# A local-attention transformer on eight cores: wqkv loaded in one piece per row block, and the W1 loop interleaved with its LayerNorm

## The reference, cut

```
x = layernorm(x + attention(x, Wq, Wkv, Wo))          # causal, 16 heads, 2048 tokens, width 1024
y = x
for l in range(2):
    h = shift_token(y)                                # columns 512..1023 shifted by one token
    q, k, v = split(h @ wqkv[l], 3)                   # 3 x 512
    q, k = rotary(l2norm(q) * qs, l2norm(k) * ks)
    y = y + local_attention(q, k, v, window 512) @ wo[l]
    h = layernorm(shift_token(y)) * g + b
    a, g = split(h @ w1[l] + b1, 2)                   # 2 x 2730
    y = y + (a * gelu(g)) @ w2[l] + b2
out = layernorm(x + y)
```

## Time and profile before

| what | us |
|---|---|
| runs | 4656.06 and 4775.8, median 4715.93 |
| the profiled execution | 4707.03 |
| its span, slowest core (7) | 4705.1 |
| TensorE matmuls busy | 3161.8 (67%) |
| VectorE, ScalarE, POOL busy | 1513.8 (32%), 1018.1 (22%), 408.8 (9%) |
| DMA queues | 118.13 MB moved, mean 25 GB/s |
| first QKV matmul, layers 0 and 1 | at 1350.9 and 2958.4 |
| W1 loop, half 0 and half 1 of layer 0, start | at 2293.95 and 2656.63 |
| W1 loop, half 0 and half 1 of layer 1, start | at 3905.7 and 4361.3 |

### The profile page before, as it was taken

One profiled execution on the slowest core, in us unless ns is written; L12 is line 12 of the kernel. 1 busy time (PEld: TensorE's weight loads), 2 busy tenths in 40 slices (PEclk: granted clock), 3 DMA queues, 4 the chain that ended last, 5 costly groups with the idle time before them and its releaser, 6 DMA issues.

```text
span 4705.1 us, 43223 instructions; the slowest of 8 cores (4644.6 to 4705.1 us)
## 1 busy us (share of the span) xinstructions
PE 3161.8 (67%) x11488; PEld 1080.7 (23%) x11488; DVE 1513.8 (32%) x3019; ACT 1018.1 (22%) x1209; POOL 408.8 (9%) x449
## 2 busy tenths in 40 slices
PE   3656566666436667777579696566777765884996
PEld 1212121121112222222134242122222212331341
DVE  1322322212224444444311421344444452124213
ACT  0022435355111222222110110212222211101111
POOL 0000000000022200000020020222000001100110
PEclk9866677788667755556689698676555567875786
DMA  4100000000220010001262262002000014622542
GB/s 113 22 15 0 0 1 0 0 1 0 76 41 18 12 12 1 1 1 25 27 68 25 23 60 40 6 18 23 1 1 1 1 25 49 57 45 40 52 47 56
DMA packets 212862, 118.13 MB, mean 25 GB/s; under 512 B 186364, under 2 KB 188668, under 8 KB 210576
## 3 DMA queue, kind: packets, MB, share of 16 engines
q0 software_dynamic: 203120, 81.52, 15.7%
q1 hardware_dynamic: 9504, 33.85, 2.3%
HBM read 171.25 MB, written 16.78 MB: 40 GB/s over the span
## 4 chain that ended last, share of the span: by engine, by line
PE 53%; DVE 15%; ACT 14%; issue 9%; DMA 9%; DVEq 1%; ACTq 0%; POOLq 0%; POOL 0%; SPq 0%
PE PS L1423 7%; PE PS L1383 6%; PE PS L1392 6%; ACT AR L1108 4%; PE PS L868 4%; ACT AR L588 3%; PE PS L1010 3%; DMA AR<-fw 3%; PE PS L606 3%; PE PS L560 3%; PE PS L654 2%; DMA AR<-fqkvqk 2%; PE PS L1099 2%; PE PS L922 2%; DVE AR L1118 1%
## 5 line engine op out<-in xcount | busy, mean ns | idle before, releaser
L1383 PE MATMUL PS<-AR 128*128 128x512 bf16 (+1 forms) x1408 | 580.4, 412 | 145.7 <-DVE AR L1406 78.1
L1392 PE MATMUL PS<-AR 128*128 128x512 bf16 (+1 forms) x1408 | 578.9, 411 | 0.0
L1108 ACT ACTIVATE AR<-PS 128x1024 bf16<-128x1024 f32 x224 | 229.4, 1024 | 742.2 <-PE PS L1099 533.7
L588 ACT ACTIVATE AR<-PS 128x1024 bf16<-128x1024 f32 x320 | 310.2, 1021 | 316.4 <-PE PS L560 197.8
L1423 PE MATMUL PS<-AR 128*128 128x512 bf16 (+1 forms) x1408 | 344.1, 402 | 3.8 <-ACT AR L1399 3.7
L1406 DVE SCALAR_TENSOR_TENSOR AR<-PS,FBIA,AR 128x512 bf16<-128x512 f32 (+1 forms) x176 | 132.0, 750 | 645.9 <-ACT AR L1399 256.2
L1141 PE MATMUL PS<-AR 128*65 128x512 bf16 x448 | 234.2, 625 | 100.5 <-DVE AR L1124 78.4
L868 PE MATMUL PS<-AR 128*128 128x512 bf16 x512 | 166.1, 498 | 187.4 <-DMA AR<-fqkvv 162.9
L560 PE MATMUL PS<-AR 64*128 64x512 bf16 x640 | 199.5, 488 | 136.8 <-ACT AR L588 90.3
L1399 ACT ACTIVATE AR<-PS,FBIA 128x512 bf16<-128x512 f32 (+1 forms) x176 | 121.0, 687 | 624.3 <-PE PS L1392 409.7
L606 PE MATMUL PS<-AR 128*65 128x512 bf16 x640 | 212.6, 458 | 45.6 <-DVE AR L593 45.6
(11 more groups left out here) (163 smaller groups left out, 3414.4 us busy)
## 6 DMA issues: line engine op xcount, KB each, us to landing
AR<-fw POOLq DMA_DIRECT2D x210, 256.0 KB, 4.4
XT<-xt SPq DMA_DIRECT2D x8, 1024.0 KB, 22.3
xin_spill<-XT SPq DMA_DIRECT2D x8, 1024.0 KB, 16.4
AR<-rot SPq DMA_DIRECT2D x16, 512.0 KB, 4.2
XT<-xin_spill POOLq DMA_DIRECT2D x32, 256.0 KB, 4.0
out_xt<-XT SPq DMA_DIRECT2D x32, 256.0 KB, 2.3
AR<-wkvT POOLq DMA_DIRECT2D x8, 512.0 KB, 6.1
AR<-fqkvqk POOLq DMA_DIRECT2D x16, 256.0 KB, 4.7
```

The costliest lines, as they stand in the source:

```text
L588: return eng.activation(out=pt[:, 0:1024], in_=bank(sb, 0, 1024), func=AF.Exp)
L1108: return eng.activation(out=pt[:, 0:1024], in_=bank(2, 0, 1024), func=AF.Exp)
L1383: return eng.matmul(out=bank(ch, 0, 512, 0, hcs), lhsT=w[:, 0:hcs], rhs=h2n_t(dc)[:, ch * 512:(ch + 1) * 512], start=(dc == 0), stop=(dc = ...
L1392: return eng.matmul(out=bank(2 + ch, 0, 512, 0, hcs), lhsT=w[:, 0:hcs], rhs=h2n_t(dc)[:, ch * 512:(ch + 1) * 512], start=(dc == 0), stop=( ...
```

## The change

The diff has three parts. The two host arrays `fqkvqk` and `fqkvv` become one, `fqkv`, and each row block of wqkv is loaded at once, 1536 columns. The body of the LayerNorm becomes a function `f3ln(ch)`, the matmuls and the gelu with its multiply become `w1mm(c, ch)` and `w1post(c, ch)`, their contents as before; the loop calls them in another order: the first group (0, 0) stands between the two LayerNorm chunks, and group (c, 0) stands ahead of group (c-1, 1). `w1load` runs two chunks ahead in place of three: chunks 0 and 1 before the loop, chunk `c+2` in iteration `c`.

```
     for dc in range(DC):
         def ld(eng, dc=dc):
-            return eng.dma_start(out=wqkv_t(dc, 0, 1024),
+            return eng.dma_start(out=wqkv_t(dc, 0, 1536),
                                  in_=fqkv_d[l, dc * 128:(dc + 1) * 128, :])
-        B.emit("G", ld, dma="g_fqkv", writes=(f"fqkv.{dc}", "r_wqkv", "r_w1b0", "r_w1b1", "r_w1b2", "r_wqspare"), tag=f"{L}ldqk{dc}")
-    for dc in range(DC):
-        def ld(eng, dc=dc):
-            return eng.dma_start(out=wqkv_t(dc, 1024, 512),
-                                 in_=fqkvv_d[l, dc * 128:(dc + 1) * 128, :])
-        B.emit("G", ld, dma="g_fqkv", writes=(f"fqkvv.{dc}", "r_wqkv", "r_w1b0", "r_w1b1", "r_w1b2", "r_wqspare"), tag=f"{L}ldvv{dc}")
+        B.emit("G", ld, dma="g_fqkv", writes=(f"fqkv.{dc}", "r_wqkv", "r_w1b0", "r_w1b1", "r_w1b2", "r_wqspare"), tag=f"{L}ldqkv{dc}")
...
-    for c in range(3):
+    for c in range(2):
         w1load(0, c)
...
-        for ch in range(2):
+        def f3ln(ch, hh=hh, hc0=hc0):
             c0 = hc0 + ch * 512
...
-        if hh == 1:
-            for c in range(3):
-                w1load(hh, c)
-        for c in range(NHC):
...
+        if hh == 1:
+            for c in range(2):
+                w1load(hh, c)
+        f3ln(0)
+        w1mm(0, 0)
+        f3ln(1)
+        for c in range(NHC):
+            if c >= 1:
+                w1mm(c, 0)
+            w1post(c, 0)
+            if c >= 1:
+                w1mm(c - 1, 1)
+                w1post(c - 1, 1)
+            if c + 2 < NHC:
+                w1load(hh, c + 2)
             if hh == 0 and 11 + c < NHC:
                 w2load(11 + c)
+        w1mm(NHC - 1, 1)
+        w1post(NHC - 1, 1)
```

More of the change, by code:

```diff
@@ L319, in build_program @@
         for l in range(2):
-            ffn_layer(ctx, l, fqkv_d, fqkvv_d, fwo_d, fw1_d, fw2_d, rot_d, BASE,
+            ffn_layer(ctx, l, fqkv_d, fwo_d, fw1_d, fw2_d, rot_d, BASE,
                       fin=final_chunk if l == 1 else None)
@@ L741, in phaseA, with ffn_layer @@
     emit_ln_tail(NCH - 1)
-def ffn_layer(ctx, l, fqkv_d, fqkvv_d, fwo_d, fw1_d, fw2_d, rot_d, base, fin=None):
+def ffn_layer(ctx, l, fqkv_d, fwo_d, fw1_d, fw2_d, rot_d, base, fin=None):
     B = ctx["B"]
@@ L1370, in ffn_layer, with w1mm @@
                        tag=f"{L}3x3.{hh}.{ch}.{dc}")
-        if hh == 1:
-            for c in range(3):
-                w1load(hh, c)
-        for c in range(NHC):
+        def w1mm(c, ch, hh=hh):
             hcs = HCS[c]
             buf = c % 3
[L1379 to L1414, removed]
@@ new lines, in w1mm, with mma, mmg @@
+            for dc in range(DC):
+                def mma(eng, dc=dc, ch=ch, buf=buf, hcs=hcs):
+                    w = ar[:, o_w1 + buf * 2048 + dc * 128: o_w1 + buf * 2048 + dc * 128 + 128]
+                    return eng.matmul(out=bank(ch, 0, 512, 0, hcs),
+                                      lhsT=w[:, 0:hcs],
+                                      rhs=h2n_t(dc)[:, ch * 512:(ch + 1) * 512],
+                                      start=(dc == 0), stop=(dc == DC - 1))
+                B.emit("T", mma, reads=(f"w1a.{buf}", f"h2n.{dc}", "r_hT", f"r_w1b{buf}"),
+                       writes=(f"ps{ch}",), tag=f"{L}wa.{hh}.{c}.{ch}.{dc}")
+                def mmg(eng, dc=dc, ch=ch, buf=buf, hcs=hcs):
+                    w = ar[:, o_w1 + buf * 2048 + 1024 + dc * 128: o_w1 + buf * 2048 + 1024 + dc * 128 + 128]
+                    return eng.matmul(out=bank(2 + ch, 0, 512, 0, hcs),
+                                      lhsT=w[:, 0:hcs],
+                                      rhs=h2n_t(dc)[:, ch * 512:(ch + 1) * 512],
+                                      start=(dc == 0), stop=(dc == DC - 1))
+                B.emit("T", mmg, reads=(f"w1g.{buf}", f"h2n.{dc}", "r_hT", f"r_w1b{buf}"),
+                       writes=(f"ps{2 + ch}",), tag=f"{L}wg.{hh}.{c}.{ch}.{dc}")
@@ new lines, in w1post, with gel, umul @@
+        def w1post(c, ch, hh=hh):
+            hcs = HCS[c]
+            def gel(eng, ch=ch, hcs=hcs, c=c):
+                return eng.activation(out=GG[0:hcs, :],
+                                      in_=bank(2 + ch, 0, 512, 0, hcs),
+                                      func=AF.Gelu, bias=B1G(l, c)[0:hcs, 0:1])
+            B.emit("S", gel, reads=(f"ps{2 + ch}",) + FBR, writes=("gg", "r_v"),
+                   tag=f"{L}gg.{hh}.{c}.{ch}")
+            def umul(eng, c=c, ch=ch, hcs=hcs):
+                return eng.scalar_tensor_tensor(
+                    out=u_t(c)[0:hcs, ch * 512:(ch + 1) * 512],
+                    in0=bank(ch, 0, 512, 0, hcs), scalar=B1A(l, c)[0:hcs, 0:1],
+                    in1=GG[0:hcs, :], op0=ALU.add, op1=ALU.mult)
+            B.emit("V", umul, reads=(f"ps{ch}", "gg", "r_v") + FBR,
+                   writes=(f"u.{c}", u_alias[c]),
+                   tag=f"{L}um.{hh}.{c}.{ch}")
```

8 lines of the change are left out of this document (3 added, 5 removed).

## The result

The changed kernel takes 4751.23 us (median of 12 runs, 4716.22 to 4840.70); the kernel before, run beside it, 4691.96 us (10 runs, 4656.06 to 4812.94). The ratio is 1.0137, 95% interval 1.0094 to 1.0181: slower by 1.4%, within the 2% that I called no change, and inside the range of 4670 to 4800, 31 us above the forecast of 4720. In some executions the cores of one die run at a lower granted clock; the ratios leave these executions out, the medians hold them.

What follows compares the result with a forecast made beforehand. TensorE bounds nearly everywhere, POOL's weight loads in three places. Layer 0 +26 (-21 + 11 + 36) and layer 1 +2 (-23 + 11 + 14) gave 4735, the shorter run 4706; the middle, 4720, was forecast, range 4670 to 4800.

Steps and rivals of the forecast that it cites:

- A: Merged 1536-column wqkv loads at each layer's head: 21 us less in layer 0, 23 less in layer 1, taken as -44.
- The rival in which time goes by bytes: Merged wqkv loads at the layer heads bring little, -5 us, 4774 on the profiled time; chance 0.08.
- Its bound of 8 us for layer 1: If time went by bytes alone, merged wqkv loads would gain only 8 us in layer 1's head, none in layer 0's.
- 2% mark of 4802: Total time, reckoned on the profiled execution, beyond which the kernel counts as slower by over 2%; chance 0.13.
- B: First W1 group ahead of the second LayerNorm chunk: hidden, paid back, second cold start; +1.8 in each of four halves, +7.
- C: Two chunks of lead in the W1 loops: TensorE stalls some 3 us every second chunk, 17.9 us a pair.
- the lead of three gave 13.8 us for 10.0 and hid it: In the old W1 loop, three chunks of lead left 13.8 us to cover a load needing about 10.0.
- the rival of cold stalls: Every W1 loop stall leaves TensorE cold: 19.0 a pair, +10 per half 1, +4 per half 0, 4748; chance 0.18.
- the 190 to 200 that it named as the sign: Half 1 of layer 0 at 190 to 200 us would show the stalls from two chunks of lead.
- The sum: Whole kernel: +26 in layer 0 and +2 in layer 1 give 4735; +50 on the shorter run gives 4706; middle 4720.
- +14: Growth of layer 1's half 1 from 186.5 us: 195.7 if the clock comes back, 206 if it stays.

Runs made afterwards that it cites:

- part A alone: The kernel before with only the wqkv loads merged, one of 1536 columns per row block: 4619.14 us, ratio 0.9895.
- The last runs: Own semaphores for W1's second halves in the changed kernel (4630.69 us), and for these and wqkv loads on the kernel before with merged loads, lead two (4553.16 us).
- the run of B alone: The kernel before with only the first W1 group placed between the two LayerNorm chunks: 4713.91 us, ratio 1.0061.
- lead 2 alone: The kernel before with W1 loads emitted two chunks ahead in place of three, order of the groups as before: 4644.51 us, ratio 0.9912.
- the version with lead 2: The kernel before with merged wqkv loads and W1 loads two chunks ahead, old group order: 4578.97 us, ratio 0.9833; with own keys for g, w2 and wqkv 4571.31 us.
- the semaphore of its own: The changed kernel with a region key and semaphore of its own for the second half of each W1 load: median 4630.69 us of four executions.
- the fastest version: The kernel before with merged wqkv loads, two chunks of lead in the old order, and own semaphores for W1's second halves and each layer's wqkv loads: 4553.16 us, ratio 0.9639.

## Why the prediction was right

**A, taken as -44, was -44** (-22.2 and -21.8). In part A alone it was -42. The step from 4.1 us (1024 columns) and 5.6 (2048) to 4.85 for 1536 columns held: 4.92. Layer 0's loads that meet the spill took 13 us where the smaller ones took 12, so there too the number of loads counted for more than their bytes. The rival in which time goes by bytes is out. Its bound of 8 us for layer 1 does not follow from the rows: if time went by bytes alone, the same bytes in fewer loads would gain nothing; neither figure would have moved the forecast. (The prediction's 2% mark of 4802 should read 4801.) The last runs correct the picture behind it: much of a load's 4.9 us is waiting for a landing that nothing needed.

**B, taken as +1.8 a half, was 0 to +4.3, mean +2.4** in the run of B alone. That the mean is so near is in part luck, since a half moves by more than that from one execution to the next; that B neither gains 5 us a half nor costs as much is what the runs bear out. TensorE's timeline, layer 0, half 0, shows the early group, then chunk 1, then the second group:

```profile
2265.25 0.58 PE L1372 MATMUL PS<-AR 128*128 128x512 bf16 x1 [16.99 <-DVE AR L1359]
...
2269.81 0.38 PE L1381 MATMUL PS<-AR 128*128 128x512 bf16 x1
2270.12 0.38 PE L1277 MATMUL PS<-AR,CSTB 128*1 128x512 bf16 x1
...
2305.14 0.59 PE L1372 MATMUL PS<-AR 128*128 128x512 bf16 x1 [16.62 <-DVE AR L1399]
```

From first group to second it is 39.9 us. I had 40.9: 35.4 from 2258.57 to 2293.95, 0.3 earlier and 5.25 later. Both groups start cold, as I had said.

**C was the right mechanism with the right price, under a wrong name.** The prediction headed it "Two chunks of lead in place of three" and closed with "the lead of three gave 13.8 us for 10.0 and hid it". The working below that heading is of the interleaved order (the buffer is freed by group (c-1,1), and only (c+1,0) and (c,1) lie between that and the need), and it holds. But lead 2 alone costs next to nothing in half 1, and saves 25 us or more in each half 0, a gain that the kernel before had open and that I had not looked for: I read the wait of the gelu in the earlier trace rows as the w2 load's, and not as that of the W1 load ahead of it on POOL.

**The size of C.** With B inside I had +36 for a half 1 at the higher clock and +11 for a half 0; measured are +41.4 and +35.7, +14.0 and +11.2. In layer 0, half 1, of core 7 six pairs from 2690.00 to 2804.18 take 19.0 us each, and I had 17.9. Five of the six have a stretch at the lower clock (the one from 2690.00 starts cold behind the 16.6 us of the LayerNorm) where I took one in two (0.7 us of the 1.1, at the 2.1 us each that I had); the load takes 9.6 us from issue to TensorE's start (2719.85 to 2729.44) where I had 9.41. The 0.2 us that remain I cannot place. So that stretch ran nearer the rival of cold stalls, which had 19.0 for a pair. Further on the stalls are shorter, and over the whole half six of twelve lost clock, as forecast. The wait for fw that was to be 20 to 35 us in half 1 came to 29.4 and 34.6. Half 1 of layer 0, counted as the prediction counted it, went from 159.8 to 201 (159.8 + 41.4), just above the 190 to 200 that it named as the sign and below the 205 that would have spoken for cold stalls throughout.

**The sum.** By cores at the higher clock the prediction had -44 + 2 x 47 = +50, and the stages give +58. It was the choice between this and the profiled execution that took me away from it: there layer 1 ran at 0.81, and I took +14 only, for a clock that might come back. The windows of the changed kernel, layers 0 and 1, half 1, on the same core 7:

```profile
2690.00:2887.00 197.00, 165.02 (x688) 69.61 (x688) 31.51 (x42) 29.54 (x43) 33.20 (x38) 0.92 0.55 49
4409.00:4595.00 186.00, 149.15 (x627) 63.07 (x625) 29.26 (x39) 27.10 (x40) 32.21 (x37) 0.93 0.57 51
```

Here layer 1 was at 0.93 on that core, about as layer 0, while cores 4 and 5 were the low ones: their half 1 took 284.6 and 281.3 us, against 256.2 and 259.2 on cores 6 and 7 before, so +25 where the clock was low in both. Which cores have the low clock in a half changed from the one execution to the other, and no run shows that the kernel sets it. The term built on it, +14 for what was +36, was worth 11 us of the 31 by which 4720 fell short, since I took the middle of the two sums. Some 8 are C, sized too small (the stages give +58, not +50). Another 10 are the base: I set out from the middle of 4656 and 4707, and the kernel before has a median of 4692 over ten runs. The reasons for "within 2%" held: two large terms, each of the sign and nearly the size forecast. That the total fell into the range also took some luck, since the median of 4751 holds executions up to 4841.

Left open is in part why half 1 of layer 0, with the same W1 loop, takes 235 us on some pairs of cores and 247 on others of the same execution (cores 4 and 5 against 0 and 1 in the run of A alone). It is not the clock, 0.84 to 0.86 on all four from 2554 to 2800. In that half TensorE's a line waits 14.2 us for fw on core 0 and 4.7 on core 4, and POOL waits 88.7 against 76.8 us for the landings that stand before its 19 second loads. So the chained loads land later on the one than on the other, and with semaphores of their own all eight cores take 229 to 230 us. Why they land later no run shows. Nor was it taken apart why w2 loads with keys of their own shorten half 0 of the changed kernel by 13 us, while the version with lead 2 did not get shorter by them.

## What to carry to other kernels

A change of order is priced by the buffer that it keeps busy: ask which group reads it last, and how much work then lies between that and the next need; the number of chunks of lead alone says little, and a longer lead can even be later when it asks for the buffer that was just read. Before moving work to cover a load, look at the load: if it is a chain of transfers that wait for each other's landing and nothing needs that order, give them semaphores of their own. Keys are not enough, and the profile's line "idle, ended by DMA" on the issuing engine shows whether the edit took.

## What the runs showed of the hardware

- **Landings, not bytes, paced these loads.** One load of 1536 columns behind another takes 4.92 us when it waits for the landing. Eight issued together took 27 us from first issue to the first matmul, 3.4 each. Each was slower on its own (a median of 21.1 us from issue to landing in the table of DMA issues, against 4.7 to 5.2 chained), and the sum quicker:

```profile
AR<-fqkv POOLq DMA_DIRECT2D x16, 384.0 KB, 21.1
```

- **How long a stall was did not settle the clock.** In the twelve rows above, the starts after 3.02 us of idle and more were cold, and so was that after 2.26; those after 2.54, 2.64 and 2.81 were warm, and after 2.23 the clock fell only within the 4 us behind the start. On the kernel before 2.82 was warm and 2.90 cold. In half 1 of layer 1 of the changed kernel TensorE started after 3.44 us, and the 4 us behind it ran at the full clock, 1.00 (2.4 GHz):

```profile
4567.19 0.38 PE L1372 MATMUL PS<-AR 128*128 128x512 bf16 x1 [3.44 <-DMA AR<-fw]
...
4567.19:4571.19 4.00, 4.00 (x19) 1.86 (x20) 0.00 (x0) 0.28 (x1) 0.87 (x1) 1.00 0.38 39
```

Six of the twelve stalls of layer 0, half 1, lost clock, and a model that makes half of such stalls cold, at 2.1 us each, came out near over that half.

- **Closing the stalls gave the matmuls back as well.** The mean matmul of the a line went from 411 ns in the changed kernel to 392 with the semaphore of its own, and to 383 in the fastest version. The 412 of the kernel before is that of core 7, at 0.81 in its last half; on cores 0 to 5 it has 393 to 395.

```profile
L1377 PE MATMUL PS<-AR 128*128 128x512 bf16 (+1 forms) x1408 | 539.5, 383 | 88.5 <-DVE AR L1359 64.4
```
